# Moving the second layer's key copies to one DMA issuer, and the result stores ahead of them

## The chip, the cores and the metric

The kernel runs on one core of one Trainium2 chip. The metric is the device time of one execution in microseconds (us). Three executions of the kernel before gave a median of 767.23 us (765.45 to 767.73). The profile is of one further execution, which took 766.16 us; its span, from the first to the last instruction, is 764.4 us.

## What is computed

The reference is two cross-attention layers, one after the other, for each of 16 samples. A sample has 112 query rows of width 320 and a context of 375 rows of width 192.

```python
# layer 0: 8 heads of 40; the last 4 context rows are handled apart
enc, ca = ctx[:, :371], ctx[:, 371:]
hs  = mha(x @ Wq, enc @ Wk, enc @ Wv)
q1  = einsum('btc,th->bch', ca, Wq_ca)[:, indices]      # 112 rows
hs1 = mha(q1, x, x)
hs2 = mha(hs1 @ Wq, ca @ Wk_ca, ca @ Wv_ca)
x   = (hs + hs2) @ Wout + b_out + x
# layer 1: 20 heads of 16, all 375 context rows
x   = mha(x @ Wq1, ctx @ Wk1, ctx @ Wv1) @ Wo1 + bo1 + x
```

All is float32 in and out. The kernel splits the operands of most products into a rounded part ("hi") and its rest ("lo"), so that a product takes several passes.

## The kernel before, in words

The whole run is a software pipeline over the samples. The loop `for t in ITERATIONS` (t = 0 to 17) is written out on every engine, and each t has seven slots (`SLOTS`). In a slot, TensorE (PE) does the scores of one group of four heads, the shifted scores and the attention of the group two slots before, and some "units" from the table `UNITS` (L46): projections, transposes and small products, each into one of two PSUM banks `bankX` used in turn. Iteration t works on several samples at once:

- layer 0 of sample t: scores in slots 0 and 1; layer 1 of sample t-1: scores in slots 2 to 6 (`SCORED`, L77). In iteration 16, where there is no layer 0, layer 1 begins a slot earlier, in slot 1.
- the keys of layer 1 of sample t, units K1_0, K1_1, K1_2, at the end of slot 1 and in slots 2 and 3; the keys of layer 0 of sample t+1, K0_0 to K0_2, in slots 3 and 4
- q0 of sample t+1 (slot 1, phase 2), out1 of sample t-2 (slot 4, phase 2: the final result), out0 of sample t (slot 5, phase 2)

The keys leave PSUM through ScalarE (ACT) and VectorE (DVE) as hi and lo parts into the tile `stage` (`k1_hi`, `k1_lo`, `k0_hi`, `k0_lo`). From there DMAs copy them, head by head, into the stacked tiles `k0_stack` and `k1_stack` (two buffers, by the parity of the sample), which the score products read.

- Layer 0's keys: 9 copies, `stack_k0` (L337), issued by SyncE (SP) after K0_2 is drained (L342).
- Layer 1's keys: 24 copies, 8 steps r of 3 (`k1_moves`, L294). Steps 0 to 3 move three chunks of 16 partitions (70.5 KB a copy), steps 4 to 7 two chunks (47 KB a copy). SP issues steps 0 to 3, `stack_k1` (L350 to L358); GpSimd (POOL) issues steps 4 to 7, its own `stack_k1` (L486 to L492), with its own semaphores `k1_stacked_pool`.

Who waits for layer 1's copies of sample b: PE before the first layer 1 scores of that sample (L1137 to L1139, the matmuls of L1147), in iteration b+1, slot 2; and ACT before it writes K1_0 of sample b+1 into `stage` (L611, L612, the activation of L614), at nearly the same moment.

The order on SP in iteration t (L383 to L401): load `gst` (waits for out0 of t-1); load x and ca of sample t+2, then the context of t+2, then xp of t+1; the 9 copies of layer 0's keys of t+1; the 12 copies of layer 1's keys of t; and last the store of the result of sample t-2 (L401), which waits for out1 of t-2 (L400). An instruction that waits on SP holds up all behind it.

The order on POOL in iteration t (L516 to L544): expand_w2 and split_ctx for t+1 (L457, L451); its 12 copies; normalise2 of t+1 (L464); add_bias1 of t (L472), which writes `x1b` of t and therefore waits until the store of sample t-2 has landed (L471); add_bias0 (L481); split_ca and split_x of t+2 (L420, L434). The unit q0 of sample t+2 on PE, in iteration t+1, waits for split_x (L1027).

Of the kernel before, what the change touches and what calls it, by code (L numbers as in the profile page):

```python
# [36 lines left out]
SLOT_L1 = 2  # L37
M_ROW0, M_ROW1 = 3 * D0, 3 * D1
ROWS1 = 64 + 3 * D1
DMAS_K0, DMAS_K1 = 9, 12  # L40
MT_BUFS = 4


# [68 lines left out]
def xattn_kernel(nc, xT, xpad, ctxT, caS, caT, w_all, w_ca, wqT, bd96, consts, bias, out):  # L112
    g_rows = nc.dram_tensor("g_rows", [B, 3, 32, HID], F32, kind="Internal").ap()

    with ExitStack() as ctx:
# [130 lines left out]
        xp_loaded = sem("xp_loaded")  # L246
        k0_stacked = sem("k0_stacked")
        k1_stacked = [sem(f"k1_stacked{i}") for i in range(2)]
        k1_stacked_pool = [sem(f"k1_stacked_pool{i}") for i in range(2)]
        scores_done = sem("scores_done")  # L250
        max_done = sem("max_done")
        mT_done = sem("mT_done")
# [53 lines left out]
        @block.sync  # L306
        def _(sp):
            xT_cols = xT.rearrange("b p c q -> p b (c q)")
            caS_cols = caS.rearrange("b p q -> p b q")
            xp_cols = xpad.rearrange("b p n -> p b n")  # L310
            ctx_cols = ctxT.rearrange("b p c n -> p b (c n)")

            def load_weights(i):
                sp.dma_start(raw_weights[i], weight_part(i, w_all)).then_inc(w_loaded[i], 16)

            def load_x(b):
                if b > 0:
                    sp.wait_ge(x_split, b)
                    sp.wait_ge(ca_split, b)
                    sp.wait_ge(unit_filled, filled("W2", b - 1))  # L320
                sp.dma_start(x_raw[:, :, :].rearrange("p c q -> p (c q)").unsqueeze(1), xT_cols[:, b:b + 1, :])\
                    .then_inc(x_loaded, 16)
                sp.dma_start(ca_raw[:, :].unsqueeze(1), caS_cols[:, b:b + 1, :]).then_inc(ca_loaded, 16)

            def load_ctx(b):
                if b > 0:
                    sp.wait_ge(ctx_split, b)
                sp.dma_start(ctx_raw[:, :, :].rearrange("p c n -> p (c n)").unsqueeze(1), ctx_cols[:, b:b + 1, :])\
                    .then_inc(ctx_loaded, 16)

            def load_xp(b):
                if b > 0:
                    sp.wait_ge(xb_ready, b)
                    sp.wait_ge(unit_filled, filled("PV2", b - 1))
                sp.dma_start(xp[:, :].unsqueeze(1), xp_cols[:, b:b + 1, :]).then_inc(xp_loaded, 16)

            def stack_k0(b, rs):  # L337
                if b == 0:
                    sp.wait_ge(zeroed, 2)
                else:  # L340
                    sp.wait_ge(st_done, NUMBER[0, b - 1, 1] + 1)
                sp.wait_ge(bank_drained[bank("K0_2", b)], drained("K0_2", b))  # L342
                for r in rs:
                    nch = 3 if r < 2 else 2
                    for part, src in enumerate((k0_lo, k0_hi, k0_hi)):
                        to = D0 * part
                        sp.dma_start(k0_stack[to:to + D0, r:r + 3 * (nch - 1) + 1:3, :].bitcast(F32),
                                     src[D0 * r:D0 * r + D0, 0:nch, :]).then_inc(k0_stacked, 16)

            def stack_k1(b, rs):  # L350
                if b < 2:
                    sp.wait_ge(zeroed, 5)
                else:
                    sp.wait_ge(st_done, NUMBER[1, b - 2, G1 - 1] + 1)
                sp.wait_ge(bank_drained[bank("K1_2", b)], drained("K1_2", b))
                for r in rs:
                    for dst, src in k1_moves(b, r):
                        sp.dma_start(dst, src).then_inc(k1_stacked[b % 2], 16)  # L358

            sp.dma_start(cst[:, :], consts).then_inc(const_loaded, 16)  # L360
            load_weights(1)
            load_ctx(0)
            sp.dma_start(bd[:, :, :], bd96).then_inc(bd_loaded, 16)
            load_x(0)
            load_weights(0)
            load_weights(4)
            load_weights(3)
            load_xp(0)
            load_weights(2)
            load_weights(5)  # L370
            sp.dma_start(bias_sb[:, :, :], bias).then_inc(bias_loaded, 16)
            load_ctx(1)
            load_x(1)
            stack_k0(0, range(3))
            for m in range(4):
                sp.wait_ge(g_split, m + 1)
                for j in range(2):
                    rows = slice(4 * (2 * m + j), 4 * (2 * m + j) + 4)
                    for part, src in enumerate((g_lo, g_hi, g_hi)):
                        sp.dma_start(g_rows[:, part, rows, :],  # L380
                                     src[64 * j:64 * j + 64, m, :].bitcast(F32)).then_inc(g_stored, 16)

            for t in ITERATIONS:  # L383
                if t < B:
                    if t > 0:
                        sp.wait_ge(unit_filled, filled("out0", t - 1))
                    else:
                        sp.wait_ge(g_stored, 16 * 24)
                    sp.dma_start(gst[:, :].bitcast(F32), g_rows[t].rearrange("a r n -> (a r) n"))\
                        .then_inc(g_loaded, 16)  # L390
                if t + 2 < B:
                    load_x(t + 2)
                    load_ctx(t + 2)
                if t + 1 < B:
                    load_xp(t + 1)
                    stack_k0(t + 1, range(3))
                if t < B:
                    stack_k1(t, range(4))
                if 0 <= t - 2:
                    sp.wait_ge(bank_drained[bank("out1", t - 2)], drained("out1", t - 2))  # L400
                    sp.dma_start(out[t - 2], x1b[t % 2][:, :]).then_inc(out_stored[t % 2], 16)  # L401
            for i in range(2):
                sp.wait_ge(out_stored[i], 16 * (B // 2))

        @block.gpsimd
        def _(pool):
# [76 lines left out]
                    xp[:, :].rearrange("p (h d) -> p h d", h=H0)[:, :, 0:D0],  # L483
                    bias_sb[:, 0, :].rearrange("p (h d) -> p h d", h=H0), ALU.add).then_inc(xb_ready, 1)

            def stack_k1(b, rs):  # L486
                if b >= 2:
                    pool.wait_ge(st_done, NUMBER[1, b - 2, G1 - 1] + 1)
                pool.wait_ge(bank_drained[bank("K1_2", b)], drained("K1_2", b))
                for r in rs:  # L490
                    for dst, src in k1_moves(b, r):
                        pool.dma_start(dst, src).then_inc(k1_stacked_pool[b % 2], 16)  # L492

            nc.gpsimd.memset(qn[:, :].bitcast(F32), 0.0).then_inc(zeroed, 1)
            nc.gpsimd.memset(k0_stack[:, :, :].bitcast(F32), 1.0).then_inc(zeroed, 1)
            nc.gpsimd.memset(odd_rows[:, :], 1.0).then_inc(q1T_zeroed, 1)
# [19 lines left out]
            for t in ITERATIONS:  # L516
                if t + 1 < B:
                    expand_w2(t + 1)
                    split_ctx(t + 1)
                if t == 0:  # L520
                    pool.wait_ge(ctx_split, 2)
                    nc.gpsimd.memset(q1T[:, :, :, :].bitcast(F32), 0.0).then_inc(q1T_cleared, 1)
                    nc.gpsimd.memset(k1_stack[1][:, :, :].bitcast(F32), 1.0).then_inc(zeroed, 1)
                    pool.wait_ge(g_stored, 16 * 24)
                    nc.gpsimd.memset(k1_stack[0][:, :, :].bitcast(F32), 1.0).then_inc(zeroed, 1)
                    pool.wait_ge(w_split, 6)
                    for i in range(2):
                        nc.gpsimd.memset(v1[i][:, :, :], 0.0).then_inc(v_cleared, 1)
                        pool.wait_ge(v_cleared, 2 + i)
                        nc.gpsimd.memset(v1[i][:, :, :].rearrange("p k (h d) -> p k h d", d=32)[:, :, :, D1:D1 + 1],  # L530
                                         1.0).then_inc(zeroed, 1)
                if t == 0:
                    normalise2(1)
                if t < B:
                    stack_k1(t, range(4, 8))
                if 0 < t < B - 1:
                    normalise2(t + 1)
                if t < B:
                    add_bias1(t)
                if t + 1 < B:  # L540
                    add_bias0(t + 1)
                if t + 2 < B:
                    split_ca(t + 2)
                    split_x(t + 2)  # L544

        @block.scalar
        def _(act):
# [46 lines left out]
            def unit(name, b):  # L594
# [14 lines left out]
                if kind == "K1":  # L609
                    if i == 0 and b >= 1:  # L610
                        act.wait_ge(k1_stacked[(b - 1) % 2], 16 * DMAS_K1 * ((b - 1) // 2 + 1))  # L611
                        act.wait_ge(k1_stacked_pool[(b - 1) % 2], 16 * DMAS_K1 * ((b - 1) // 2 + 1))  # L612
                    rows = P if i < 2 else 64
                    nc.scalar.activation(k1_hi[0:rows, i, :].bitcast(F32R), X[0:rows, 0:SKP], ACT.Copy)\  # L614
                        .then_inc(k1_rounded, 1)
# [325 lines left out]
        def _(pe):  # L941
# [183 lines left out]
            def scores(g, pair):  # L1125
# [10 lines left out]
                if pair == 0 and layer == 1:  # L1136
                    if k == 0:  # L1137
                        pe.wait_ge(k1_stacked[b % 2], 16 * DMAS_K1 * (b // 2 + 1))
                        pe.wait_ge(k1_stacked_pool[b % 2], 16 * DMAS_K1 * (b // 2 + 1))  # L1139
                    pe.wait_ge(bank_drained[bank(f"q1T_{k // 2}", b)], drained(f"q1T_{k // 2}", b))  # L1140
                for j in range(2):
                    h = GROUP * k + 2 * pair + j
# [188 lines left out]
```

## Time and profile before

| | before |
|---|---|
| median of 3 runs | 767.23 us |
| the profiled execution: time / span | 766.16 / 764.4 us |
| PE busy | 707.8 us (93%) |
| DVE, ACT, POOL busy | 62%, 53%, 39% |
| layer 1 copies by SP (L358) | 192 issues |
| layer 1 copies by POOL (L492) | 192 issues, 96.2 us of POOL |
| mean granted clock of TensorE | 0.98 of full |

Times in the profile are counted in us from the start of the span. A duration of a DMA instruction on SP or POOL (`SPq`, `POOLq` or a `DMA_DIRECT2D` row) is the time its issue takes on the issuing engine; "to landing" is from the start of the issue to the end of the data transfer. Matmuls overlap: the next begins before the modelled end of the one before it. Idle time in brackets is followed by what ended it.

### The profile page before, as it was taken

What the parts mean: (1) busy time and instruction counts of PE and PEld (TensorE: products, weight loads), DVE (VectorE), ACT (ScalarE), POOL (GpSimd) and SP (SyncE); (2) the same over time, 40 slices, a digit from 0 to 9 for tenths busy, and PEclk for the clock granted to TensorE, in tenths of its full rate; (3) what the DMA queues carried; (4) which work ended last, traced back from release to release, by engine and by line L of the source; (5) the groups of instructions that cost most, each with busy time, mean ns of one, the idle gap of its engine ahead of it and who ended that gap; (6) DMA issues with size and microseconds to landing.
All of it is one profiled execution on the core that took longest, in us unless ns stands there. A gap on an engine that the chain in (4) does not pass through costs nothing. (4 is left out here: it accounts for less than half of the span.)

```text
span 764.4 us, 18175 instructions
## 1 busy us (share of the span) xinstructions
PE 707.8 (93%) x6916; PEld 614.1 (80%) x6916; DVE 472.7 (62%) x1028; ACT 403.6 (53%) x923; POOL 294.3 (39%) x401
## 2 busy tenths in 40 slices
PE   6878899999999999999999999999999999999975
PEld 4667788888888888888888888888888888888763
DVE  1554475757666575756666575766657575666662
ACT  1455365555555555556555555555555555654432
POOL 5387444414244443515344441524444250530300
PEclk9979999999999999999999999999999999999997
DMA  9433534352615334251524335262433425051400
GB/s 322 140 124 80 125 85 93 81 114 60 139 58 126 75 100 92 64 138 47 135 74 104 76 84 118 59 138 59 122 64 106 94 71 138 16 137 31 85 2 15
DMA packets 52387, 72.45 MB, mean 95 GB/s; under 512 B 12128, under 2 KB 44256, under 8 KB 52304
## 3 DMA queue, kind: packets, MB, share of 16 engines
q1 hardware_dynamic: 44832, 60.34, 31.1%
q0 software_dynamic: 6144, 9.25, 6.4%
q10 hardware_dynamic: 1328, 1.71, 0.6%
q8 instruction: 57, 0.93, 0.5%
q14 instruction: 26, 0.21, 0.1%
HBM read 20.60 MB, written 4.26 MB: 33 GB/s over the span
## 5 line engine op out<-in xcount | busy, mean ns | idle before, releaser
L768 DVE TENSOR_REDUCE negmax<-bankS 112x2 f32<-112x750 f32 (+1 forms) x224 | 208.7, 932 | 59.4 <-PE bankS L1147 32.7
L492 POOL DMA_DIRECT2D k_stack<-stage x192 | 96.2, 509 | 137.6 <-DVE stage L804 120.0
L572 ACT ACTIVATE arena<-bankST 125x1344 f32<-125x1344 f32 x80 | 103.4, 1293 | 31.8 <-PE bankST L1181 31.8
L1213 PE MATMUL bankO<-arena,v 125*32 125x112 f32 (+2 forms) x2688 | 107.9, 265 | 6.2 <-ACT arena L572 4.6
L1213 PEld LDWEIGHTS bankO<-arena,v 125*32 125x32 f32 (+2 forms) x2688 | 81.7, 118 | 29.0 <-issue 12.7
L472 POOL TENSOR_TENSOR x1b<-x,bias_sb 112x320 f32<-112x320 f32 x16 | 13.8, 863 | 232.5 <-DMA out<-x1b 204.9
L1147 PE MATMUL bankS<-k_stack,q1T 112*112 112x376 f32 x320 | 87.7, 355 | 3.5 <-DVE negmax L768 3.0
L993 PE MATMUL bankX<-ctx_hi,WH 128*120 128x376 f32 (+2 forms) x192 | 70.3, 366 | 0.8 <-DVE qn L760 0.3
L993 PE MATMUL bankX<-WH,ctx_hi 128*125 128x320 f32 x192 | 66.2, 345 | 0.0
L1181 PE MATMUL bankST<-q1T,k_stack 112*125 112x224 f32 x480 | 65.7, 272 | 0.3 <-DMA q1T<-mT 0.3
L993 PE MATMUL bankX<-ctx_hi,WL 128*120 128x376 f32 (+2 forms) x192 | 65.5, 341 | 0.0
L1181 PEld LDWEIGHTS bankST<-q1T,k_stack 112*125 112x125 f32 x480 | 61.9, 188 | 1.5 <-DMA q1T<-mT 1.0
L993 PE MATMUL bankX<-WL,ctx_hi 128*125 128x320 f32 x192 | 58.5, 312 | 0.0
L1147 PEld LDWEIGHTS bankS<-k_stack,q1T 112*112 112x112 f32 x320 | 49.5, 177 | 7.8 <-DVE negmax L768 5.5
L824 DVE TENSOR_SCALAR q1T<-bankX,odd_rows 128x448 fp32r<-128x448 f32 (+1 forms) x48 | 29.1, 606 | 42.6 <-ACT q1T L661 42.1
L590 ACT ACTIVATE arena<-bankX,negmax 112x112 f32<-112x112 f32 x128 | 43.5, 353 | 22.6 <-DVE negmax L832 22.4
L993 PE MATMUL bankX<-WH,act_hi 128*112 128x320 f32 x144 | 46.7, 325 | 3.3 <-DVE act_hi L861 1.4
L774 DVE CAST mT<-bankO 4x112 fp32r<-4x112 f32 x112 | 29.0, 259 | 30.5 <-PE bankO L1160 30.5
L1175 PEld LDWEIGHTS bankST<-q0T,k_stack 121*125 121x125 f32 (+1 forms) x384 | 46.2, 188 | 0.0
L620 ACT ACTIVATE stage<-bankX 120x376 fp32r<-120x376 f32 (+1 forms) x48 | 23.2, 483 | 43.3 <-PE bankX L993 41.5
L1175 PE MATMUL bankST<-q0T,k_stack 121*125 121x112 f32 (+1 forms) x384 | 44.9, 266 | 0.0
L993 PE MATMUL bankX<-WL,act_hi 128*112 128x320 f32 x144 | 44.8, 311 | 0.0
(139 smaller groups left out, 1535.0 us busy)
## 6 DMA issues: line engine op xcount, KB each, us to landing
k_stack<-stage SPq DMA_DIRECT2D x96, 176.2 KB
k_stack<-stage SPq DMA_DIRECT2D x192, 70.5 KB, 2.6
k_stack<-stage POOLq DMA_DIRECT2D x192, 47.0 KB, 2.0
ctx_raw<-in_ctxT SPq DMA_DIRECT2D x16, 376.0 KB, 3.3
k_stack<-stage SPq DMA_DIRECT2D x48, 117.5 KB
xp<-in_xpad SPq DMA_DIRECT2D x16, 224.0 KB, 3.4
x_raw<-in_xT SPq DMA_DIRECT2D x16, 168.0 KB, 2.3
out<-x1b SPq DMA_DIRECT2D x16, 140.0 KB, 2.8
```

The source lines that it names most:

```text
L492: pool.dma_start(dst, src).then_inc(k1_stacked_pool[b % 2], 16)
L572: nc.scalar.activation(dst[0:KC], bankST[0:KC, :, 0:GROUP * SQ], ACT.Exp).then_inc(exp_done, 1)
L590: last = nc.scalar.activation(prob2[0:SQ, h, :], X[0:SQ, (h % 4) * SQ:(h % 4 + 1) * SQ], ACT.Exp, bias=negmax2[:, h:h + 1], accum_out=sum2 ...
L620: nc.scalar.activation(k0_hi[0:rows, i, :].bitcast(F32R), X[0:rows, 0:SKP], ACT.Copy)\
L768: nc.vector.tensor_reduce(negmax[:, n % 2, 2 * pair:2 * pair + 2], bankS[0:SQ, :, 0:keys], axis=AX, op=ALU.max, negate=True).then_inc(max_ ...
L774: nc.vector.tensor_copy(mT[:, n % MT_BUFS, :], bank_mT).then_inc(mT_copied, 1)
L824: nc.vector.tensor_scalar(q1T[:, 4 * i:4 * i + g, 1, :], X[:, 0:g * SQ].rearrange("p (h q) -> p h q", h=g), odd_rows[:, :], None, ALU.mult ...
L993: last = nc.tensor.matmul(dst, lhs, rhs, start=(n == 0), stop=(n == len(passes) - 1))
L1147: last = nc.tensor.matmul(bankS[0:SQ, j, 0:SKP], q1T[0:ROWS1, h // 2, h % 2, :], k1_stack[b % 2][0:ROWS1, h // 2, :], start=True, stop=True)
L1175: last = nc.tensor.matmul(bankST[0:keys, c, SQ * j:SQ * j + SQ], k0_stack[0:M_ROW0 + 1, h, KC * c:KC * c + keys], q0T[0:M_ROW0 + 1, h, :], ...
L1181: last = nc.tensor.matmul(bankST[0:KC, c, 2 * SQ * pair:2 * SQ * pair + 2 * SQ], k1_stack[b % 2][0:ROWS1, 2 * k + pair, KC * c:KC * c + KC ...
L1213: last = nc.tensor.matmul(dst, v, src[0:keys, c, SQ * j:SQ * j + SQ], start=(c == 0), stop=(c == NKC - 1))
```

## The change

SP issues all eight steps of layer 1's copies (24 issues), POOL none; the second pair of semaphores goes, and with it one wait on ACT and one on PE. On SP the store of sample t-2, with the wait ahead of it, moves from behind layer 1's copies to ahead of them. What is copied, and who needs it, is the same.

```diff
-DMAS_K0, DMAS_K1 = 9, 12
+DMAS_K0, DMAS_K1 = 9, 24
...
-        k1_stacked_pool = [sem(f"k1_stacked_pool{i}") for i in range(2)]
...
                 if t + 1 < B:
                     load_xp(t + 1)
                     stack_k0(t + 1, range(3))
-                if t < B:
-                    stack_k1(t, range(4))
                 if 0 <= t - 2:
                     sp.wait_ge(bank_drained[bank("out1", t - 2)], drained("out1", t - 2))
                     sp.dma_start(out[t - 2], x1b[t % 2][:, :]).then_inc(out_stored[t % 2], 16)
+                if t < B:
+                    stack_k1(t, range(8))
...
-            def stack_k1(b, rs):
-                if b >= 2:
-                    pool.wait_ge(st_done, NUMBER[1, b - 2, G1 - 1] + 1)
-                pool.wait_ge(bank_drained[bank("K1_2", b)], drained("K1_2", b))
-                for r in rs:
-                    for dst, src in k1_moves(b, r):
-                        pool.dma_start(dst, src).then_inc(k1_stacked_pool[b % 2], 16)
...
-                if t < B:
-                    stack_k1(t, range(4, 8))
...
-                        act.wait_ge(k1_stacked_pool[(b - 1) % 2], 16 * DMAS_K1 * ((b - 1) // 2 + 1))
...
-                        pe.wait_ge(k1_stacked_pool[b % 2], 16 * DMAS_K1 * (b // 2 + 1))
```

## Rows read from the trace of the kernel before

**Rows 1.** The page: busy us of each engine, share of the span, instructions.

```profile
PE 707.8 (93%) x6916; PEld 614.1 (80%) x6916; DVE 472.7 (62%) x1028; ACT 403.6 (53%) x923; POOL 294.3 (39%) x401
```

**Rows 2.** Waits of PE and SP: engine, line, releaser: us in total, times, longest.

```profile
PE bankX L993 <- POOL x_hi L434: 3.5, 8, 0.7
...
SPq L342 <- DVE stage L809: 205.6, 15, 21.7
```

**Rows 3.** SP in iteration 7: start, duration, engine, line, operation, tiles, count.

```profile
366.75 8.45 SPq L347 DMA_DIRECT2D k_stack<-stage  x9
375.30 8.61 SPq L358 DMA_DIRECT2D k_stack<-stage  x12
383.96 0.58 SPq L401 DMA_DIRECT2D out<-x1b  x1
```

**Rows 4.** POOL at the end of iteration 7, same columns, idle time before.

```profile
386.75 0.86 POOL L472 TENSOR_TENSOR x1b<-x,bias_sb 112x320 f32<-112x320 f32 x1 [17.54 <-DMA out<-x1b]
```

**Rows 5.** PE and DVE around the same turn of the pipeline.

```profile
374.97 0.49 DVE L855 TENSOR_TENSOR x<-bankX,xb 112x320 f32<-112x320 f32 x1 [0.38 <-PE bankX L993]
...
391.53 0.37 PE L993 MATMUL bankX<-WH,x_hi 128*112 128x320 f32 x1 [0.45 <-POOL x_hi L434]
...
395.20 0.51 PE L1147 MATMUL bankS<-k_stack,q1T 112*112 112x376 f32 x2
```

**Rows 6.** SP's shortest and longest burst of L358 (16 in all).

```profile
244.16 7.74 SPq L358 DMA_DIRECT2D k_stack<-stage  x12
...
77.43 8.69 SPq L358 DMA_DIRECT2D k_stack<-stage  x12
```

**Rows 7.** Issue durations (ns min/median/max) and landings: L358, L347, then L492.

```profile
L358 SPq DMA_DIRECT2D k_stack<-stage x192: 585/597/1487, 77.4 to 715.3; - x192
...
DMA to landing us min/median/max: 2.4/2.6/4.4
...
L347 SPq DMA_DIRECT2D k_stack<-stage x144: 767/780/1793, 24.1 to 680.5; - x144
...
L492 POOL DMA_DIRECT2D k_stack<-stage x12: 504/504/543, 361.5 to 367.0; - x12
...
DMA to landing us min/median/max: 1.9/2.0/2.0
```

**Rows 8.** The first iterations: SP, then PE.

```profile
67.43 9.89 SPq L347 DMA_DIRECT2D k_stack<-stage  x9
...
106.89 8.47 SPq L347 DMA_DIRECT2D k_stack<-stage  x9
...
80.76 0.93 PE L1144 MATMUL bankS<-k_stack,q0T 120*112 120x372 f32 x2 [3.13 <-issue]
...
91.83 0.51 PE L1147 MATMUL bankS<-k_stack,q1T 112*112 112x376 f32 x2
...
133.43 0.50 PE L1147 MATMUL bankS<-k_stack,q1T 112*112 112x376 f32 x2
```

**Rows 9.** The last iterations: SP, PE, DVE.

```profile
672.79 8.46 SPq L347 DMA_DIRECT2D k_stack<-stage  x9
...
707.17 8.67 SPq L358 DMA_DIRECT2D k_stack<-stage  x12
...
699.12 0.51 PE L1147 MATMUL bankS<-k_stack,q1T 112*112 112x376 f32 x2
...
714.76 0.49 DVE L867 TENSOR_TENSOR x1b<-bankX,x1b 112x320 f32<-112x320 f32 x1 [0.74 <-PE bankX L993]
...
728.43 0.57 PE L1147 MATMUL bankS<-k_stack,q1T 112*112 112x376 f32 x2 [0.45 <-DVE q1T L824]
```

**Rows 10.** Stretches: length, PE busy (instructions), granted clock, DMA share, GB/s.

```profile
74.00:76.00 2.00, 1.56 (x12) 1.00 1.01 227
80.00:84.00 4.00, 3.24 (x13) 0.57 0.71 119
84.00:90.00 6.00, 5.37 (x47) 1.00 0.58 116
```

## Prediction

> **What bounds the kernel now.** The page first: PE is busy 93% of the span, no other engine over 62% [rows 1]. So PE sets the pace, and what counts is where PE waits and what the change makes it wait for. The waits of each engine come second. In the steady part of the run one wait of PE belongs to the parts that the change touches: q0's matmuls wait for POOL's split_x, 8 times, 3.5 us in all [rows 2]. SP is not short of time as a whole: it waits 205.6 us for the last layer 0 key, 15 times [rows 2]. But inside an iteration its order decides. Third, the timelines of SP, POOL and PE side by side for one iteration show a loop. Layer 0's keys are drained at 366.75, SP issues 9 copies, then 12 copies, and only then the store, at 383.96 [rows 3]. POOL has been idle for 17.5 us when the store lands and it starts add_bias1 at 386.75 [rows 4]; the four operations behind it end with split_x, and PE's q0 starts at 391.53 after 0.45 us of idle time caused by split_x [rows 5]. From there PE comes back to layer 0's keys. So SP's burst, the store's landing and POOL's chain take just a little longer than PE's own work in 8 of the iterations.
>
> **What the change takes away.** The store of t-2 goes ahead of the burst. After the 9 copies SP is at 375.30 [rows 3]; the store would be issued there, not 8.66 us later. It would land at about 378.1 (383.96 to 386.75 is 2.8 us [rows 3, 4]); out0, which add_bias1 also needs, is drained at 374.97 + 0.49 = 375.46 [rows 5]. POOL's chain moves forward by 8.6 us and the wait for split_x, at most 0.7 us [rows 2], goes away. Its worth is the idle time, 3.5 us, and for each of the 8 waits the 0.16 us by which a matmul normally starts before the modelled end of the one before it: 3.5 + 1.3 = 4.8 us. POOL's 12 issues, 6 us of POOL time for each sample, free nothing else: in the steady part PE waits for no other operation of POOL, and the time goes into POOL's own idle time. Term a: -4.8 us.
>
> **What the change adds.** SP's burst for a sample has 24 copies. 12 copies take 7.74 to 8.69 us, 16 bursts with a mean of 8.3 [rows 6]; the median issue is 0.597 us, and some single ones take up to 1.487 [rows 7]. The other 12 copies have two chunks and not three. No row shows SP issuing that shape. The nearest is L347, in which three of nine copies have two chunks: its minimum is 0.767 and its median 0.780 [rows 7], so the shape with fewer chunks is not issued faster. I take the same price. From the first issue to the last: 2 x 8.28 + 0.05 - 0.60 = 16.0 us (14.9 to 16.9 from the two ends of rows 6). Landing takes 2.6 in the median and up to 4.4 [rows 7]; I take 2.7, and 0.1 for the waiting engine to start. So data are ready 16.0 + 2.8 = 18.8 us after the first copy is issued (17.7 to 19.8), where now it is some 10.5.
>
> Who needs them is PE, before the first L1147 of a sample, and ACT at the same place. In the steady part, from the first layer 0 copy: need at 395.20 - 366.75 = 28.45 us [rows 3, 5], less the 0.6 us that term a removes from that stretch: 27.9. Arrival: 8.55 for the 9 copies, 0.64 for the store, 18.8: 28.0. The cover is used up to the last tenth. The margin is -0.1 with a spread of about 0.5 (two bursts, each with its stalls). Where a burst is late PE stands and all behind it moves by as much; where it is early nothing is gained. The mean of the late part is 0.28 us (for a normal spread of 0.5 around 0.1), times 12 iterations (t = 2 to 13). Term b: +3.4 us (0 at 14.9 us a burst, 12 at 16.9).
>
> The ends are worse, since iterations there are shorter or the order bites:
> - Sample 0: layer 0's copies start at 67.43 and take 9.89 us, while POOL's 12 are under way [rows 8] and the DMA engines are fully busy [rows 10]. Without POOL's I take 8.55. Ready at 67.43 + 8.55 + 18.8 = 94.8, needed at 91.83 [rows 8]. Term c: +3.0 (1.9 to 5.4). The 3.13 us for which PE now waits for layer 0's keys at 80.76 [rows 8] will shrink, but it only makes PE arrive earlier at the later wait.
> - Sample 1: no store yet. Ready 8.55 + 18.8 = 27.35 after 106.89, needed 133.43 - 106.89 = 26.5 [rows 8]. Term d: +0.8 (0 to 1.8).
> - Sample 14: iteration 15 has no q0, so the need comes at 699.12 - 672.79 = 26.3 [rows 9] against 28.0. Term e: +1.7 (0.6 to 2.7).
> - Sample 15: there are no layer 0 copies ahead, so now the burst starts at 707.17 [rows 9]. After the change the store of sample 13 stands before it and waits for out1, drained at 714.76 + 0.49 = 715.25 [rows 9]. 24 copies are queued on SP behind this wait, and PE behind them. Ready at 715.25 + 0.65 + 18.8 = 734.7, needed at 728.43 [rows 9]. Term f: +6.3 (5.2 to 7.4). Nothing later absorbs it: each further score waits for the one before.
>
> Then the clock. After PE's 3.13 us of idle time at 80.76 [rows 8] the granted clock of 80 to 84 is 0.57 [rows 10]: mostly the lower level, 1.2 GHz, before it is full again. Such a stretch of some 3.4 us costs PE-bound work half of it. The stalls of terms c and f should bring one each: 1.6, and 1.0 at the end, where PE is not the only limit. Term g: +2.6 (0 to 5).
>
> In the timelines SP's other work keeps its cover. The gst, x, context and xp loads slip by some 8 us into the next iteration, before a stretch in which SP waits for K0_2 (13.7 us a time [rows 2]); gst is needed only at out0. No wait is added anywhere that had none; two are removed on engines where they were already met.
>
> **Sum.** -4.8 + 3.4 + 3.0 + 0.8 + 1.7 + 6.3 + 2.6 = +13.0 us. Against the profiled execution's own 766.2 (span 764.4) this is 779.2; the median of the runs is 1.0 us above that execution, so 780.2, put at 780.
>
> **A rule of the skill.** POOL's 12 two-chunk copies of one burst landed 2.0 us after issue, SP's three-chunk copies in a median of 2.6 [rows 7]. The Trainium skill, DMA: Bandwidth & Descriptors, section Latency and other measured facts, puts the first byte of the SP and ACT path at about 0.6 us and that of the GpSimd path at about 1 us, so by the page moved copies land sooner. By that rule the last copies would land in about 1.6 us and the sum would be near +5. The rows show the opposite order, though for different shapes.
>
> **The rivals.**
> 1. The moved copies land sooner than those that SP issues now. The last copy of a burst has two chunks, and those land in 2.0 us for POOL [rows 7]; then data are ready 0.8 us earlier. Terms: a -4.8, b +0.5, c +2.2, d 0, e +0.9, f +5.5, g +2.3: +6.6, so 774. For it: fewer bytes. Against: POOL's path is another. The page named above would have this too. Chance 0.15.
> 2. Not slower: the two-chunk copies are issued cheaply. Place: steps 4 to 7 of the burst on SP. The lowest issue of any row is 0.585 [rows 7] for this line, so this needs a price that no row shows; at some 0.4 us each 12 of them save about 2.9 us. Then b, d and e are gone, c is near 0, f is 3.4 and only a stays against it: -1.4, so 766. It decides from about 0.2 us saved a copy; below, the two ends outweigh a. Chance 0.12, two thirds of it within 0.3%.
> 3. A queue that fills. L347's slowest issue is 1.793 [rows 7], so issues can be held up. If 24 in a row are held to 0.81 each, the later half costs 2.0 us more: b 25, c 5, d 2.8, e 3.7, f 8.3: +43, so 810. Against: a burst of 12 right behind the 9 shows no growth, 8.61 us [rows 3]. Chance 0.08.
> 4. The gain of term a does not come, since PE then waits for another input of q0: +17.8, so 785. Chance 0.08.
>
> **How the numbers follow.** The forecast as worked out, 772 to 788 with its bounds, has 0.52; the rivals 0.15, 0.12, 0.08, 0.08; 0.05 is left for what I do not see. The range 769 to 790 leaves out rivals 2 and 3. Within 0.3% of 767.2 (764.9 to 769.5) is about what measurements of this kernel cannot tell from no change. Faster 0.05, same 0.11, slower 0.84.
>
> **What would show it.** In the changed trace: the store at about 375.3 of a comparable iteration and POOL's add_bias1 some 8 us earlier, no wait of q0 for split_x (term a); bursts of 24 in 15.5 to 17.4 us, each two-chunk issue near 0.6 (b to f); PE waits before the first layer 1 scores of samples 0, 1, 14 and 15 of 3 (or more, since PE comes earlier), 0.8, 1.7 and 6.3 us, and small ones in some of the others; the granted clock at the lower level behind the first and the last. The prediction fails if issues of two chunks cost under 0.4 us, if a burst stretches beyond 18 us, or if PE has work to put into the last wait.

## The result and the profile after

The changed kernel took 780.22 us in the median of four runs (778.14 to 783.10), the kernel before 767.48: the ratio is 1.017, with a 95% interval from 1.013 to 1.021, that is 13 us more. The forecast was 780.

| | before | after |
|---|---|---|
| median | 767.48 us | 780.22 us |
| span of the profiled execution | 764.4 | 777.9 |
| PE busy | 707.8 us (93%) | 710.9 us (91%) |
| POOL busy | 294.3 us (39%) | 198.6 us (26%) |

The first view is the page of the changed kernel; the lines of code have moved up by 1 to 13 (L1147 is now L1134, L358 is L357, L401 is L398). It answers to [rows 1]: PE runs the same 6916 matmuls in a longer span.

```profile
PE 710.9 (91%) x6916; PEld 617.4 (79%) x6916; DVE 473.6 (61%) x1028; ACT 404.1 (52%) x923; POOL 198.6 (26%) x209
```

The waits of PE, in the columns of [rows 2], show the exchange. The wait of q0's matmuls for POOL's split_x is gone from the list. In its place stands a wait that the kernel before did not have at all: L1134, the first layer 1 scores of a sample, 9 times and once more, 15.3 us together.

```profile
PE bankS L1134 <- issue: 9.8, 9, 5.1
...
PE bankS L1134 <- DMA k_stack<-stage: 5.5, 1, 5.5
```

Of one turn in the middle, SP, POOL and PE answer to [rows 3 to 5]. The nine copies end, the store goes out at 380.21 and not 8.7 us later, add_bias1 follows at 383.56, and q0 starts without a wait. The burst of 24 ends at 397.96, and gst is issued.

```profile
371.67 8.50 SPq L346 DMA_DIRECT2D k_stack<-stage  x9
380.21 0.48 SPq L398 DMA_DIRECT2D out<-x1b  x1
380.81 17.15 SPq L357 DMA_DIRECT2D k_stack<-stage  x24
398.00 0.58 SPq L388 DMA_DIRECT2D gst<-g_rows  x1
...
383.56 0.87 POOL L471 TENSOR_TENSOR x1b<-x,bias_sb 112x320 f32<-112x320 f32 x1 [9.92 <-DMA out<-x1b]
...
395.86 0.31 PE L981 MATMUL bankX<-WH,x_hi 128*112 128x320 f32 x1
...
399.61 0.56 PE L1134 MATMUL bankS<-k_stack,q1T 112*112 112x376 f32 x2
```

From the first of the nine to the first layer 1 scores are 399.61 - 371.67 = 27.94 us. The cover was put at 27.9 and the arrival at 28.0; in this turn the keys came just as PE got there.

The first layer 1 scores of samples 0, 1, 14 and 15 in PE's timeline answer to [rows 8, 9]; the number in brackets is PE's idle time.

```profile
91.46 0.94 PE L1134 MATMUL bankS<-k_stack,q1T 112*112 112x376 f32 x2 [5.05 <-issue]
...
138.28 0.57 PE L1134 MATMUL bankS<-k_stack,q1T 112*112 112x376 f32 x2 [0.98 <-issue]
...
705.67 0.57 PE L1134 MATMUL bankS<-k_stack,q1T 112*112 112x376 f32 x2 [0.64 <-issue]
...
739.45 0.94 PE L1134 MATMUL bankS<-k_stack,q1T 112*112 112x376 f32 x2 [5.48 <-DMA k_stack<-stage]
```

What releases "issue" waits is told by the landings: in 14 of the 16 samples the last copy lands 0.09 us before these scores start (in samples 4 and 6 there were 0.6 and 0.7 us to spare). The last burst stands behind the store, which waits for out1 of sample 13:

```profile
721.30 0.33 SPq L398 DMA_DIRECT2D out<-x1b  x1
721.73 16.08 SPq L357 DMA_DIRECT2D k_stack<-stage  x24
...
720.78 0.49 DVE L855 TENSOR_TENSOR x1b<-bankX,x1b 112x320 f32<-112x320 f32 x1 [0.73 <-PE bankX L981]
```

The price of the copies, in the columns of [rows 7] (the second shape, with two chunks, is in the same row):

```profile
L357 SPq DMA_DIRECT2D k_stack<-stage x384: 585/594/1816, 74.0 to 737.2; - x192
...
DMA to landing us min/median/max: 2.1/2.5/3.7
```

and the page's landings of the two shapes, three chunks and two:

```profile
k_stack<-stage SPq DMA_DIRECT2D x192, 70.5 KB, 2.6
k_stack<-stage SPq DMA_DIRECT2D x192, 47.0 KB, 2.2
```

The clock after the two long idle times, in the columns of [rows 10]: PE is idle from 86.4 to 91.46 and from 734.0 to 739.45, and the granted clock is at the lower level (0.50, which is 1.2 GHz) from 90.8 to 101.0 and from 735.9 to 742.7. Of these stretches PE works through 9.5 us and 3.3 us; the rest falls into its idle time. A further stretch of 3.4 us follows at 749.5.

```profile
91.00:101.00 10.00, 9.54 (x53) 9.05 (x55) 4.17 (x8) 4.00 (x13) 0.00 (x0) 0.50 0.35 97
101.00:111.00 10.00, 9.36 (x83) 8.37 (x79) 6.98 (x17) 5.84 (x16) 0.13 (x1) 1.00 0.00 0
...
736.00:742.00 6.00, 2.55 (x10) 0.50 0.20 40
```

### The profile page after: what moved, and what is told of

Read it like the earlier page. It is cut to its first block, busy times and chain, and to the rows that moved or that the text cites. A ratio compares the mean times of both kernels' runs of the same rounds, so it can differ in the third digit from the quotient of the medians.

```text
span 777.9 us, 18145 instructions
## 1 busy us (share of the span) xinstructions
PE 710.9 (91%) x6916; PEld 617.4 (79%) x6916; DVE 473.6 (61%) x1028; ACT 404.1 (52%) x923; POOL 198.6 (26%) x209
## 4 chain that ended last, share of the span: by engine, by line
PE 67%; ACT 12%; DVE 8%; issue 4%; SPq 2%; POOL 1%; ACTq 0%; DMA 0%; POOLq 0%
PE bankX L981 28%; PE bankO L1200 8%; PE bankST L1168 7%; ACT arena L561 6%; PE bankS L1134 6%; PE bankST L1162 5%; ACT arena L579 3%; DVE q1T L812 2%; DVE negmax L756 2%; PE bankX L1094 2%; PE bankX L1101 2%; SPq L357 2%; PE bankS L1131 2%; PE bankX L1063 2%; ACT q1T L649 2%
## 5 line engine op out<-in xcount | busy, mean ns | idle before, releaser
L1134 PE MATMUL bankS<-k_stack,q1T 112*112 112x376 f32 x320 | 90.2, 363 | 18.1 <-issue 9.8
L463 POOL TENSOR_TENSOR arena<-arena,rsum 112x896 f32<-112x896 f32 x16 | 27.0, 1685 | 254.8 <-DVE rsum L860 254.8
L1134 PEld LDWEIGHTS bankS<-k_stack,q1T 112*112 112x112 f32 x320 | 49.5, 180 | 25.6 <-issue 19.3
L602 ACT ACTIVATE stage<-bankX 128x376 fp32r<-128x376 f32 (+1 forms) x48 | 23.1, 482 | 54.3 <-PE bankX L981 29.3
L456 POOL TENSOR_TENSOR w2bd<-w2s,cst 96x896 fp32r<-96x896 f32 x16 | 29.9, 1871 | 70.7 <-DVE w2s L748 70.7
L792 DVE TENSOR_TENSOR stage<-bankX,stage 128x376 fp32r<-128x376 f32 (+1 forms) x48 | 26.2, 546 | 33.7 <-ACT stage L602 32.9
```

What stands on the lines that cost most here:

```text
L456: nc.gpsimd.tensor_tensor(w2bd[:, :, :], w2s[:, :].bitcast(F32).unsqueeze(1).broadcast_to((96, H0, SQ)), mask96.unsqueeze(2).broadcast_to( ...
L463: nc.gpsimd.tensor_tensor(prob2[0:SQ], prob2[0:SQ], rsum2[:, :].unsqueeze(2).broadcast_to((SQ, H0, SQ)), ALU.mult).then_inc(prob2_ready, 1)
L1134: last = nc.tensor.matmul(bankS[0:SQ, j, 0:SKP], q1T[0:ROWS1, h // 2, h % 2, :], k1_stack[b % 2][0:ROWS1, h // 2, :], start=True, stop=True)
```

## The experiments

The theory to be tested: the change is two changes with opposite signs. The store ahead of the copies takes the loop through split_x off PE's path (a gain); 24 issues in a row on one engine make layer 1's keys late (a loss), most at the two ends. Its rivals: that the gain comes from freeing GpSimd; that the keys are late because the DMA engines cannot move them faster, not because SP cannot issue them faster; and that the middle of the run costs nothing. Ratios are to the kernel before, on the same chips.

### The store first, the copies shared as before (e1_store_first)

```diff
-                if t < B:
-                    stack_k1(t, range(4))
                 if 0 <= t - 2:
                     sp.wait_ge(bank_drained[bank("out1", t - 2)], drained("out1", t - 2))
                     sp.dma_start(out[t - 2], x1b[t % 2][:, :]).then_inc(out_stored[t % 2], 16)
+                if t < B:
+                    stack_k1(t, range(4))
```

> The kernel before with one edit: on SP the store of sample t-2 stands ahead of SP's 12 key copies; GpSimd keeps its 12. My theory: the order of the store alone is worth the whole wait of q0 for split_x, 4.8 us less, so about 762.7 against 767.5; q0 waits for split_x no more; the burst of 12 is ready some 8 us before it is needed in the middle, and in sample 15, where it now stands behind out1 of sample 13, about 726.5 against a need at 728.4, so no new wait. Rival A: the gain in the changed kernel came from taking the copies off GpSimd, not from the order; then this kernel stays at 767. Rival B: the store's wait at the end costs as it does in the changed kernel; then 767 to 768 with a wait ahead of the first layer 1 scores of sample 15.

Measured: 760.63 us, ratio 0.990 (0.989 to 0.992), 7.4 us less than the kernel before and 20 less than the changed one. Rival A falls: GpSimd keeps its copies and the gain is there. Rival B falls too: the last burst of 12 lands at 717.3, 2.4 us before it is needed. In PE's timeline every turn that ends at samples 2 to 13 takes 43.3 us, where the same turns of the kernel before take 43.3 to 44.1. The gain is larger than the 4.8 expected. In the trace, the first layer 1 scores of samples 0, 1 and 14 answer to [rows 8, 9]:

```profile
87.94 0.51 PE L1147 MATMUL bankS<-k_stack,q1T 112*112 112x376 f32 x2
...
129.57 0.51 PE L1147 MATMUL bankS<-k_stack,q1T 112*112 112x376 f32 x2
...
690.92 0.50 PE L1147 MATMUL bankS<-k_stack,q1T 112*112 112x376 f32 x2
```

From 129.57 to 690.92 are 561.35 us, and from 133.43 to 699.12 were 565.69: 4.3 us less in the middle of this pair of traces. The spans differ by 6.6 us (764.4 and 757.8). A further 3.9 us of that lie ahead of sample 0's first layer 1 scores, which start at 87.94 and not at 91.83 [rows 8]. The edit changes no order there, since the first store goes out in iteration 2, so this part is not shown to be an effect of it; at the end 2.1 us go the other way.

### The kernel before, a second trace (before_again)

> The kernel before once more, for a second trace of it. In the first trace q0 waited for split_x in 8 iterations, 3.5 us in all, and the kernel with the store first gained 7 us in the median, not 4.8. Theory: the wait varies from execution to execution, since the loop goes through SP's burst, whose issues are held up at random places by up to 1 us; then a second trace has a sum other than 3.5, somewhere from 3 to 8 us. Rival: the wait is a fixed 3.5 us in 8 iterations, and the other 2 us come from the start of the run.

Measured: one execution of 768.19 us, with PE's wait:

```profile
PE bankX L993 <- POOL x_hi L434: 4.1, 8, 1.0
```

With the lost overlap this trace gives 5.8 us where the first gave 4.8, counted in both from the starts of q0 and of the matmul before it. So the wait varies, as the theory says, but two traces do not bring it to the 7.4 us between the medians. What makes up the rest (1.5 to 2.5 us) is open. The rival's start of the run is not refuted: sample 0's first layer 1 scores start at 91.83 and 91.34 in the two traces of the kernel before and at 87.94 in that of the store-first kernel. A stretch of 3.4 us at the lower clock, near 80 us in both traces of the kernel before, is not in that of the store-first kernel, although PE waits 3.0 us at that place there too; it was not tested what that stretch depends on.

### 18 copies on SP and 6 on GpSimd, the store first (e4_eighteen_six)

```diff
-                    stack_k1(t, range(8))
+                    stack_k1(t, range(6))
...
+                    stack_k1(t, range(6, 8))
```

The first line is SP's, the last GpSimd's, which has its `stack_k1` and its semaphores again.

> The changed kernel's order (store first), but SP issues 18 of the 24 copies (steps 0 to 5) and GpSimd 6 (steps 6 and 7). My theory: the loss goes with how late the last copy is; 18 copies take 12.3 us and not 16.6, so data are ready 4 us sooner, which is more than any lateness in the middle (at most 1.2 us) and takes 4 of the 5 us at the end: about 764.5, near the kernel with 12 and 12. Rival: the loss is in proportion to the copies that SP issues (its queue slows everything); then halfway between, about 771.

Measured: 760.63 us, ratio 0.990 (0.988 to 0.993). Not halfway between 12 and 24, but equal to 12, and 4 us less than the 764.5 expected; why the expectation was too high was not traced. SP's bursts are ready 3.2 to 5.2 us before they are needed in samples 1 to 14; PE waits only for the first and the last, 0.8 and 0.5 us more than with 12. The loss is not in proportion to the issues. It begins where the keys come later than PE wants them, and the rival falls.

### All 24 copies, the store behind them (e2_keys_first)

```diff
+                if t < B:
+                    stack_k1(t, range(8))
                 if 0 <= t - 2:
                     sp.wait_ge(bank_drained[bank("out1", t - 2)], drained("out1", t - 2))
                     sp.dma_start(out[t - 2], x1b[t % 2][:, :]).then_inc(out_stored[t % 2], 16)
-                if t < B:
-                    stack_k1(t, range(8))
```

> The changed kernel, but the store stays behind the 24 copies, the order of the kernel before. My theory: the loop SP burst, store landed, add_bias1, split_x, q0, layer 0 keys gets 8.3 us longer in each turn: 8.55 + 16.6 + 2.8 + 4.8 + 19.2 = 52 us a turn where it was 43.7, over 12 turns 99 us, and some at the ends: 865 to 885. q0 waits about 8 us for split_x each time. Rival: GpSimd, freed of its 12 issues, makes good for most of it: under 800.

Measured: 890.36 us, ratio 1.159 (1.156 to 1.163). The second half of the change is what makes the first half bearable: without it the run is 110 us slower than the changed kernel. The loop is the one that was read from the trace of before, as PE's waits and a turn of SP show:

```profile
PE bankX L981 <- POOL x_hi L433: 98.9, 12, 9.1
...
418.24 8.51 SPq L346 DMA_DIRECT2D k_stack<-stage  x9
426.85 17.03 SPq L357 DMA_DIRECT2D k_stack<-stage  x24
443.93 0.58 SPq L400 DMA_DIRECT2D out<-x1b  x1
```

The waits are as expected (8.2 us each); the turns take 52 to 54 us and not 52. At the end of each of the 12 waits the granted clock is at the lower level for 6.8 or 10.2 us, of which 3 to 6 us still fall into the idle time, as in this one:

```profile
394.00:401.00 7.00, 2.92 (x20) 0.53 0.11 31
401.00:440.00 39.00, 37.81 (x396) 1.00 0.35 84
```

The four turns with 6.8 us of it take 52.7 us in the mean, the eight with 10.2 us take 53.8. The run came out 5 us above the upper end of what was expected, which had left the clock out.

### The last burst ahead of the store (e3_last_burst_early)

```diff
+                if t == B - 1:
+                    stack_k1(t, range(8))
                 if 0 <= t - 2:
                     ...
-                if t < B:
+                if t < B - 1:
                     stack_k1(t, range(8))
```

> The changed kernel, but in iteration 15 alone the 24 copies stand ahead of the store, as they did before. My theory: the store's wait for out1 of sample 13 holds the last burst up by about 8 us, which makes PE stand 5 us and then run a stretch at the lower clock; without it 5.0 us plus 1 to 2 us of clock go, so about 773.5 against 780.2. Rival: the last layer 1 scores wait for something else than the store (the length of the burst itself); then the time stays within 1 us of 780.

Measured: 774.49 us, ratio 1.010 (1.007 to 1.014), against 1.017: about 5 us back. The runs spread from 769.7 to 780.6, so the medians say little about one or two us; the trace is clearer:

```profile
732.42 0.57 PE L1136 MATMUL bankS<-k_stack,q1T 112*112 112x376 f32 x2 [0.45 <-DVE q1T L814]
```

The releaser and the 0.45 us are those of the kernel before [rows 9], and from sample 14's first scores to these are 28.75 us, where the changed kernel takes 739.45 - 705.67 = 33.78. The wait behind the store costs 5.0 us. The rival falls.

### The first burst shared (e5_first_shared)

```diff
-                    stack_k1(t, range(8))
+                    stack_k1(t, range(4 if t == 0 else 8))
...
+                    stack_k1(0, range(4, 8))
```

The last line is GpSimd's, in iteration 0 alone.

> The changed kernel, but the second half of sample 0's copies (12 of 24) goes to GpSimd again, with a semaphore of its own. My theory: in the changed kernel PE stands 5.1 us before sample 0's first layer 1 scores and the granted clock is at its lower level for the 10 us after it, which cost 4.1 us; with 12 copies the wait is gone and with it that stretch, less the 3 us that PE then waits for layer 0's keys as in the kernel before: 4 to 5 us less than the changed kernel, so about 775.5. Rival: the wait is for the transfers, not for SP's issues, and 24 copies from two issuers are no sooner: then 780.

Measured: 774.88 us, ratio 1.010 (1.006 to 1.013): 5.6 us back by the ratios. No wait before sample 0's layer 1 scores is left, the 10 us at the lower clock are gone, and a shorter stretch of 3.4 us near 80 is back together with a wait of 3.3 us for layer 0's keys. The rival falls.

### Both ends mended (e6_both_ends)

The edits of the last two together.

> Both mends of the ends in one kernel: sample 0 shared with GpSimd, and the last burst ahead of the store; 24 copies on SP in all other iterations. My theory: the gains add, since they lie 700 us apart: 5 to 6 us from the end and 4 to 5 us from the start, so about 770; what is left above the kernel with the store first and 12 and 12 (760.6) is the lateness of the bursts of samples 1 to 14, 6.4 us in the trace of the changed kernel. Rival: the middle costs nothing that can be measured and this kernel comes to 761 to 763.

Measured: 767.31 us, ratio 0.999 (0.997 to 1.001). By the ratios 13.5 us are back, where the two alone sum to 10.8 and about 10 were expected; the intervals are wide enough to cover that. The kernel still has 24 copies on SP in 14 iterations, and still stands 0.9% (6.8 us) above the kernel with the store first and 12 and 12. In the trace of the changed kernel the late part of samples 1 to 14, by the starts of the scores and of the matmul before, sums to 6.4 us. In the trace of this kernel it takes 701.33 - 91.74 = 609.6 us from sample 0's first layer 1 scores to sample 14's, where the store-first kernel takes 690.92 - 87.94 = 603.0. So the middle does cost what the lateness says, and the rival (761 to 763) falls.

### Half of the bytes (e7_half_bytes)

```diff
-   moves.append((k1_stack[b % 2][to:to + D1, r // 2:r // 2 + 4 * (nch - 1) + 1:4, :].bitcast(F32),
-                 src[D1 * r:D1 * r + D1, 0:nch, :]))
+   moves.append((k1_stack[b % 2][to:to + D1, r // 2:r // 2 + 4 * (nch - 1) + 1:4, 0:SKP // 2].bitcast(F32),
+                 src[D1 * r:D1 * r + D1, 0:nch, 0:SKP // 2]))
```

> The changed kernel, but each of the 24 copies of layer 1's keys moves only the first 188 of 376 columns: the same number of issues, half of the bytes; the second half of the keys is left out of the scores. My theory: the burst is bound by SP's issue, about 0.6 us each whatever it moves; its length stays 15 to 17.5 us and the waits of PE stay, with 0.1 to 0.3 us less in the landing: 778 to 780. Rival: the DMA engines are the limit (they were busy 60 to 70% during a burst); then the burst becomes shorter by some 3 us or more and the waits in the middle go: 768 to 772.

Measured: 781.64 us, ratio 1.018 (1.012 to 1.023), no faster than the changed kernel and above the 778 to 780 expected. The copies and the DMA share from 206 to 224 us, here and then in the changed kernel:

```profile
L357 SPq DMA_DIRECT2D k_stack<-stage x384: 585/594/1634, 73.9 to 736.2; - x192
...
DMA to landing us min/median/max: 1.9/2.1/3.5
...
206.00:224.00 18.00, 17.75 (x214) 15.71 (x208) 10.19 (x20) 10.82 (x19) 8.91 (x11) 1.00 0.28 68
```

```profile
206.00:224.00 18.00, 17.61 (x193) 15.48 (x193) 10.39 (x21) 10.84 (x19) 9.41 (x11) 1.00 0.52 98
```

The DMA engines are busy 28% and not 52% of the stretch (the expectation had put the changed kernel's share during a burst at 60 to 70%), the copies land 0.4 us sooner in the median, and the issue is 0.594 us as before, to the nanosecond. The burst is bound by SP's issue alone. The rival of the transfers falls.

### Less of a collision at the start (e8_first_pool_late)

The store-first kernel, with GpSimd's 12 copies of iteration 0 moved behind split_x of sample 2. Beside e1's edit on SP, this is GpSimd's part:

```diff
-                if t < B:
+                if 0 < t < B:
                     stack_k1(t, range(4, 8))
...
                     split_x(t + 2)
+                if t == 0:
+                    stack_k1(0, range(4, 8))
```

> The kernel with the store first and 12 and 12 copies (760.6), but in iteration 0 GpSimd issues its 12 copies after split_x of sample 2, so that they no longer share the DMA engines with layer 0's 9 copies of sample 1. My theory: those 9 copies then take 8.5 us and not 10 and land 2.6 and not 5 us after issue; PE's 3 us wait for them goes, layer 1's keys land some 3 us before they are needed: 2.5 to 3.5 us less, 757 to 758. Rival: PE's wait is set by when K0_2 is drained, not by the contention: no change, 760.6.

Measured: 756.53 us, ratio 0.985 (0.982 to 0.988). This is the fastest version: 11 us less than the kernel before, 24 less than the changed one. SP's nine copies of iteration 0 now run alone. They, PE's wait for them and sample 0's first layer 1 scores:

```profile
65.96 8.21 SPq L347 DMA_DIRECT2D k_stack<-stage  x9
...
76.85 0.56 PE L1146 MATMUL bankS<-k_stack,q0T 120*112 120x372 f32 x2 [0.70 <-issue]
...
87.34 0.57 PE L1149 MATMUL bankS<-k_stack,q1T 112*112 112x376 f32 x2 [0.59 <-DMA k_stack<-stage]
```

They took 9.89 us in the kernel before [rows 8] and 10.04 in the store-first kernel, with GpSimd's twelve beside them and, in the kernel before, a DMA share of 1.01 [rows 10]. PE's wait of 3 us for them is 0.8 us or less now. So here sharing the DMA engines did cost time, unlike in the bursts of the middle.

The collision is moved, not gone. GpSimd's copies now run beside the end of SP's first burst, whose last copy lands 5.1 us after its issue, and PE waits 0.6 us for it; the expectation had these keys some 3 us early. And the trace places only part of the gain of 4 us. From the first of the nine copies to sample 0's layer 1 scores are 21.4 us, where the store-first kernel takes 22.9. Up to sample 15's first layer 1 scores this trace is 0.8 us ahead (718.90 against 719.70). The other 2.2 us of the 3.0 between the two spans come after that, where the store-first trace spends 19.2 us at the lower clock and this one 11.8; that the edit causes this is not shown. The rival (no change) falls all the same: 760.6 and 756.5 are further apart than their runs spread.

## Why the prediction was right, step by step

| term | predicted | measured |
|---|---|---|
| a, q0's wait for split_x | -4.8 | -4.8 and -5.8 in two traces; -7.4 (6.1 to 8.5) between medians |
| b, samples 2 to 13 late | +3.4 | +4.4 (eight of twelve late, up to 1.2) |
| c, sample 0 | +3.0 | -0.4 at the scores themselves (+3.5 against the store-first trace) |
| d, sample 1 | +0.8 | +1.15 |
| e, sample 14 | +1.7 | +0.8 |
| f, sample 15 | +6.3 | +5.0 |
| g, the clock after stalls | +2.6 | +4.1 at the start, +2.5 at the end |
| sum | +13.0 | +13.5 between the spans, +12.7 between the medians |

The measured terms, with -4.8 for a, sum to 12.8; 0.7 us of the difference between the spans are not assigned. Between the medians of the store-first and the changed kernel lie 20 us, of which the measured terms b to g cover 17.6.

**Term a** held in place and sign: e1 shows it alone. Its size came from one trace, and a second trace had a larger wait. Whether all of the 7.4 us between the medians is this term is open, as said under e1.

**The burst.** Its length was put at 16.0 us from first to last issue (14.9 to 16.9); the 16 bursts took 15.2 to 17.5 with a mean of 16.3. The price of the shape that no row showed was the right one: 0.593 us in the median against 0.596 for three chunks. The landing of the last copy was 2.15 us in most bursts and not 2.7. These two errors, 0.3 and 0.55 us, have opposite signs, which is why terms b, d, e and f came within 1.3 us of the traces. Counted to the end of the last issue the longest burst took 18.05 us, just past the 18 that the prediction had named as a sign of failing; it was one burst of 16, and its sample came 0.9 us late. Rival 1 was half right, then: the moved copies do land sooner than the others, by 0.4 us in the median, but not as soon as from GpSimd (2.0 us [rows 7]) for the same shape. The Trainium skill, DMA: Bandwidth & Descriptors, section Latency and other measured facts, gives the path of SP and ACT the earlier first byte (about 0.6 us against about 1 us for GpSimd). The times here run from the start of the issue to the landing, which is more than the first byte; by them SP's path was not the faster one, and the forecast that the prediction drew from the page, a landing at about 1.6 us, did not come.

**Terms c and g** came out right only in their sum. The step that failed is the time at which sample 0's keys are ready, put at 94.8. In the trace of the changed kernel the nine copies started at 65.69 and took 8.24 us, where 67.43 and 8.55 were assumed, and from the start of the burst to the scores 17.4 us passed and not 18.8. So the scores started at 91.46, 0.4 us earlier than before and not 3.0 later. The 67.43 is the latest start of all the traces here (65.0 to 67.4); against the trace of the store-first kernel, where sample 0's scores start at 87.94, they are 3.5 us later.

But PE had arrived some 5 us earlier than before, stood for 5.05 us, and then had the lower level not for 3.4 us but for 10. From sample 0's layer 1 scores to the next q0 of the pipeline, 41.9 us passed where 37.9 had: +4.1. The clock's row that was used [rows 10] is of a shorter idle time (3.1 us). e5, which takes both away, gives 5.6 us back.

The end's 2.5 us are less sure than the start's 4.1. From sample 15's first layer 1 scores to the end of the span, the three traces with the long last wait (the changed kernel, e5, e7) take 37.4 to 39.8 us, the eight without it 35.5 to 38.1. The trace of the kernel before has 35.9, near the low end, and the store-first trace 38.1 with no long wait at all. The sum of c and g was put at 5.6 and is 6.2 by the traces, of which the end has 2.5: a lucky exchange between two terms.

**Term f** is the step that e3 undoes: 5.0 us, and the mechanism is the one named, a store with its wait ahead of a burst in the one iteration that has nothing else to do there.

**The rivals.** Cheap issues of two chunks, a queue that fills up, and a gain that does not come were all absent: the issue is 0.593 us in the median, the second twelve issues of a burst take no longer than the first (0.653 against 0.666 us in the mean), and q0 waits no more. Three of the rivals' prices do not follow from their rows: for rival 1 the rows give 2.7 - 2.0 = 0.7 us and not 0.8, for rival 2 12 x (0.597 - 0.4) = 2.4 us and not 2.9, and for rival 3 12 x 0.81 - 8.28 = 1.4 us and not 2.0. The forecast does not rest on them.

## What to carry to other kernels

When an issuing engine's instructions are counted, count the time until the last transfer of the whole burst has landed, and set it against the moment of need in each iteration, the first and the last too: up to that moment a longer burst is free (12 and 18 copies gave the same time), beyond it each further issue (0.66 us in the mean, stalls included) is paid on the critical engine: for the last sample 24 copies cost PE 4.4 us more than 18. Place a store that releases a buffer ahead of long bursts, not behind them; that order alone was worth 1% by the medians (4.3 us of it placed by the traces), and in the variant with the long burst it was worth 110 us. Where two edits come together, build each alone: here one half was a gain of 7 us and the other a loss of 20.

## What the runs showed that was not expected

**Single issues of over 1 us on SP.** A median issue is 0.594 us, but in the changed kernel 20 of 384 take 1.0 to 1.8 us. All 20 overlap a 16 KB packet of the instruction queue, which itself takes about 1 us (in the kernel before 9 of 10 do, in all eleven traces 166 of 172). In the changed kernel 17 other issues overlap one as well, and 14 of them stay under 0.7 us; of the 34 issues of 0.7 to 1.0 us only 3 overlap one. The DMA view of 210 to 212 us and the issues at the same place:

```profile
q8 instruction: 1, 0.02, 3.5%
...
L357 SPq DMA_DIRECT2D k_stack<-stage x2: 599/1042/1486, 209.7 to 210.4; - x2
```

That is a coincidence in time in every trace, not an experiment. If it is the cause, the spread of the bursts, and with it the spread of the runs where a burst has no cover, comes from code being loaded.

**A stall costs more than its length.** After idle times of about 5 us (changed kernel, e2, e3, e7) or 7 to 9 us (e2) PE's granted clock was at 1.2 GHz for 6.8 to 13.7 us, the first part of it still inside the idle time. After idle times of 3.1 to 4.0 us near 80 us it was there for 3.4 us (both traces of the kernel before, e5) or 6.8 us (e6), and after one of 3.0 us not at all (e1). In the changed kernel the 5.05 us before sample 0 were followed by a loss of 4.1 us.
